# Decoder layer with retention and a mixture of experts: the closing batch's projection to its fifth expert tile reordered, GpSimd's last products and VectorE's early plan rewritten

## The chip, the cores and the metric

One core of one Trainium2 chip runs the whole program. The metric is the device time of one execution in microseconds, as the median of several runs.

## The reference, cut to what matters

The input is x[8, 256, 128]: eight batches of 256 tokens. Three residual blocks follow one another.

```python
x = x + attention(layernorm(x))          # 16 heads of 64, causal, gated by a sigmoid, projected by Wout
x = x + retention(layernorm(x), ctx)     # 16 heads of 8, queries from x, keys and values from ctx
x = x + experts(layernorm(x))            # 12 experts 128 -> 512 -> 128, each token goes to its best 3

gate_logits = einsum('bsd,de->bse', x, Wg)
topw, sel = top_k(gate_logits, 3); topw = softmax(topw)
h = gelu(einsum('bsd,edh->ebsh', x, Wup) + bup)
y = einsum('ebsh,ehd->ebsd', h, Wdown) + bdown
out = einsum('bse,ebsd->bsd', cw, y)     # cw: topw at the chosen experts, 0 elsewhere
```

## The kernel before, in words

The program is written by hand, one instruction stream for each engine, tied by semaphores. It has two phases that overlap.

**Attention phase.** Batch b goes through eight steps s = 0 to 7, one pair of heads each. In one step TensorE does the scores of pair s, the query and key projection of pair s + 1, the turning (transposes) of the probabilities of pair s - 1 (`turn`) and the weighing of the values of pair s - 2 (`weigh`). VectorE takes the maxima of the scores (`maxima`, L1331 and L1332, into `nmx`), the ratios of sums and gates (`ratio`, L1344 to L1351; where `turned()` holds the result is `rg`, L1347, and TensorE transposes it at L983; the last batch does so from pair 2 on), and scales the weighed values (`scale_out`, L1360, into `oT`). ScalarE takes the exponentials (`probs`) and copies out of PSUM. In the same steps the batch before (`prev`) is finished: projection by Wout in step 2, first residual and its normalisation in step 3 (`x1b`, `brs`, `xn2`, L1374 and L1376), the retention state in steps 4 and 5 (`state` on TensorE, `read_state` L1407 on VectorE, `retained` on GpSimd), second residual in step 6 (`x2b`, `xc3`, again L1374 and L1376), logits and the choice of experts in step 7 and in steps 0 and 1 of the next batch (`route_a`, `choose`, `route_b`, `route_c`). Batches 1 to 6 run in a loop on each engine, the last batch (b = 7) is written out.

GpSimd holds what no other engine has time for, in one fixed order: the rotated queries (`queries`, four operations of `rotate`), the rotated keys (`keys`, four operations), the outer products of keys and values for the retention state (`products`, two operations of about 1.95 us, into `kv`, or for the last batch `kv_last`, which lies in `wkv_sb`), the sums of `retained`, the copy of the residual (`keep`), the threefold copy of the tokens (`pack`), and the scatters `send(b, n)`, n = 0 to 5, that write a batch's tokens to `tokens_by_expert` in DRAM, ordered by expert. Between the scatters stand small operations (`carry`) behind waits for VectorE, which place the scatters in time. `v_xc3`, `v_dl`, `v_nm`, `v_norm` are VectorE's semaphores: batch's xc3 ready, logit differences ready, maxima, scaled values.

**Expert phase.** The rows of `tokens_by_expert` are handled in 35 tiles: 24 of 256 rows and 11 of 128. Which expert and which rows a tile has is worked out on VectorE, as plans of small integers: the first 7 tiles (EARLY) from the counts of six batches (`early_plan`), the next 3 from those of seven (`later_plan`), the rest from all. Each plan is a chain of operations on 12 to some 170 numbers, each of which waits for the one before (`link`). Beforehand `early_plan` has three parts, run after steps 2, 3 and 5 of the last batch; the third (`first_rows`, `experts_past`, `tile_rows`, L1591 to L1606) ends with the increment of `v_first`. SyncE waits for it, then loads the tiles (`load(n)`, L440); ahead of that it stores padding rows behind each expert's region, twelve stores of 390 KB (L445).

A tile n is: `turn_tokens(n)` (TensorE, L1166, 2 transposes), a copy of them (ScalarE, `tokens_high`, L877), a copy of the expert's up weights (`up_high`, L872), `up(n)` (TensorE, L1182, 8 matmuls), `gelu(n)` (ScalarE, L855, 4 operations), `down(n)` (TensorE, L1212, 16 matmuls), `results(n)` (VectorE, L1735 and L1738) and `scatter(n)` (GpSimd, L677). up(n) and up(n - 2) share a PSUM bank, so up(n) waits for gelu(n - 2); down(n) waits for gelu(n) and for results of an earlier tile.

Tiles 0 to 4 are interleaved by hand with the end of the last batch, which has no attention left to hide in: projection (L1043), first residual, four retention states (`state(b, t, half)`, L1061 and L1062, two matmuls in all but the first two), their readings, second residual, `ffn_in` (L1075), `logits` (L1081), `counts` (L1091 to L1095), choice. Between them ScalarE must change its function table twice: from gelu's to that of the logarithm and exponential (L897) for the root (L728, L730), and back (L903), each ahead of the next gelu. LAST_CHAIN = 3 says behind which tile this happens.

The order of work that the change touches is written in TensorE's list at the end of its stream, in ScalarE's list behind `LAST_CHAIN`, in GpSimd's `batch`, `first_half` and the lines behind its loop, and in VectorE's lists of `early_plan`, `later_plan` and `results`.

## Time and profile before

| | us |
|---|---|
| median of 3 runs | 491.77 |
| lowest and highest | 487.0, 491.91 |
| the profiled execution | 489.44 |
| its span (first to last instruction) | 487.4 |
| TensorE busy in the span | 440.2 (90%) |
| VectorE | 366.6 (75%) |
| ScalarE | 324.7 (67%) |
| GpSimd | 242.3 (50%) |
| mean granted TensorE clock | 0.97 |

The profile is of one execution. Its times are counted from the first instruction; 2.0 us of the execution's time lie around the span. The last attention batch's steps 2 to 7 lie at about 294 to 333 us, the closing projection to tile 4 at 338 to 375, the other tiles up to 476, and the sum of the results behind that. A timeline row gives start, duration, engine, line, operation, what is written and read with its shape, the count, and in brackets the idle time of the engine before it with what ended it. Rows of a view that merges count their instructions.

### The profile page before, as it was taken

To read this page: it belongs to the slowest core of one execution; us is meant where nothing else is said; L and a number is where in the kernel's file an instruction comes from. 1 tells how busy PE (TensorE), PEld (TensorE's weight loads), DVE (VectorE), ACT (ScalarE), POOL (GpSimd) and SP (SyncE) were. 2 spreads that over 40 slices of the span, in tenths; PEclk is the share of its full clock that TensorE was granted. 3 is DMA by queue.
4 is the path that set the end of the run, shared out by engine and by line. 5 is a ranking of instruction groups with operands and counts; after the bars stand their busy time and mean duration, and the time that the engine had idled before them with its cause. 6 is when DMAs were issued, how large, how long until landed. Compare 5 with 4: busy or idle time off the path is not lost.

```text
span 487.4 us, 12686 instructions
## 1 busy us (share of the span) xinstructions
PE 440.2 (90%) x3562; PEld 366.9 (75%) x3562; DVE 366.6 (75%) x1291; ACT 324.7 (67%) x1041; POOL 242.3 (50%) x368
## 2 busy tenths in 40 slices
PE   6899999999999999999999999858879999888790
PEld 5677877877787887787787787547669998788790
DVE  3876688898898898898889889696776577454357
ACT  3899768776866867876867786434556756564460
POOL 4230042666558358267376565651836566564541
PEclk9999999999999999999999999788989999999896
DMA  8990111112111111111112116972011322211136
GB/s 262 370 279 3 48 26 37 38 46 48 35 49 45 36 46 51 41 42 42 47 35 57 37 36 150 198 124 57 29 50 44 101 78 70 63 48 51 49 109 242
DMA packets 53171, 39.22 MB, mean 80 GB/s; under 512 B 12063, under 2 KB 48723, under 8 KB 53132
## 3 DMA queue, kind: packets, MB, share of 16 engines
q1 hardware_dynamic: 49228, 31.75, 25.7%
q0 software_dynamic: 3472, 6.49, 4.2%
q10 hardware_dynamic: 432, 0.53, 0.3%
q8 instruction: 16, 0.26, 0.3%
q14 instruction: 23, 0.19, 0.1%
HBM read 25.59 MB, written 13.87 MB: 81 GB/s over the span
## 4 chain that ended last, share of the span: by engine, by line
PE 47%; DVE 28%; issue 10%; ACT 5%; DMA 3%; another core or an unknown queue 3%; DVEq 2%; POOL 1%; SPq 0%; ACTq 0%; POOLq 0%
PE zb L922 7%; PE ob L994 5%; PE sc L964 5%; PE xb L1068 5%; DVE scales L1350 4%; DVE nmx L1332 3%; PE ob L1212 3%; PE zb L1212 3%; PE sc L1182 2%; DVE kv_lo L1396 2%; PE tb_a L977 2%; PE tb_b L977 2%; DVE x_all L1804 2%; PE sc L958 2%
## 5 line engine op out<-in xcount | busy, mean ns | idle before, releaser
L677 POOL DMA_INDIRECT results_by_token<-y_sb,row_i x59 | 59.2, 1003 | 48.0 <-DVE y_sb L1738 19.3
L747 ACT ACTIVATE qk<-zb 128x512 f32<-128x512 f32 x64 | 38.2, 596 | 49.1 <-PE zb L922 49.0
L754 ACT ACTIVATE p_sb<-sc,nmx 128x128 f32<-128x128 f32 x128 | 47.6, 372 | 26.0 <-DVE nmx L1332 15.0
L756 ACT ACTIVATE p_sb<-sc,nmx 128x256 f32<-128x256 f32 x128 | 61.7, 482 | 0.0
L597 POOL TENSOR_TENSOR spare_p<-tri 128x1 f32<-128x1 f32 x36 | 7.1, 198 | 104.3 <-DVE xn L1425 66.0
L964 PE MATMUL sc<-qk 64*128 64x256 f32 (+1 forms) x512 | 58.5, 346 | 0.5 <-ACT qk L747 0.5
L994 PE MATMUL ob<-pT,v_sb 128*64 128x256 f32 (+1 forms) x512 | 56.0, 340 | 0.7 <-DVE oT L1360 0.7
L610 POOL DMA_INDIRECT tokens_by_expert<-packed,slot_i x48 | 47.8, 996 | 10.1 <-issue 7.5
L964 PEld LDWEIGHTS sc<-qk 64*128 64x128 f32 x512 | 46.4, 192 | 3.3 <-ACT qk L747 0.6
L994 PEld LDWEIGHTS ob<-pT,v_sb 128*64 128x64 f32 x512 | 31.3, 136 | 19.3 <-issue 8.4
L1332 DVE TENSOR_REDUCE nmx<-sc 128x2 f32<-128x512 f32 x64 | 43.6, 681 | 0.0
L922 PE MATMUL zb<-xT_hi,wqk_hi 128*128 128x256 f32 x112 | 36.6, 327 | 0.0
L855 ACT ACTIVATE hT<-sc,bup_sb 128x256 f32<-128x256 f32 (+1 forms) x72 | 26.4, 441 | 13.3 <-PE sc L1182 4.7
L764 ACT ACTIVATE pT<-tb_a 128x384 f32<-128x384 f32 (+1 forms) x64 | 33.9, 530 | 1.1 <-PE tb_b L983 0.3
L764 ACT ACTIVATE pT<-tb_b 128x384 f32<-128x384 f32 (+1 forms) x64 | 34.5, 538 | 0.0
L1212 PE MATMUL zb<-wdn_all,hT 128*128 x248 | 31.4, 276 | 2.6 <-ACT hT L855 1.4
L977 PE MATMUL tb_a<-ident,p_sb 128*128 128x128 f32 x192 | 32.6, 280 | 0.6 <-ACT pT L764 0.5
L1212 PEld LDWEIGHTS zb<-wdn_all,hT 128*128 128x128 f32 x248 | 29.8, 192 | 3.5 <-issue 3.3
L1212 PE MATMUL ob<-wdn_all,hT 128*128 x224 | 29.9, 286 | 2.7 <-ACT hT L855 2.4
L977 PE MATMUL tb_b<-ident,p_sb 128*128 128x128 f32 x192 | 31.8, 275 | 0.0
L922 PE MATMUL zb<-xT_hi,wqk_lo 128*128 128x256 f32 x112 | 31.6, 282 | 0.0
L922 PE MATMUL zb<-xT_lo,wqk_hi 128*128 128x256 f32 x112 | 31.4, 281 | 0.0
(320 smaller groups left out, 1267.8 us busy)
## 6 DMA issues: line engine op xcount, KB each, us to landing
scaleT<-scale_rows SPq DMA_DIRECT2D x102, 64.0 KB, 2.6
tokens_by_expert<-padding SPq DMA_DIRECT2D x12, 390.0 KB
xg<-tokens_by_expert SPq DMA_DIRECT2D x24, 130.0 KB
wup_all<-in_L_ffn_Wup SPq DMA_DIRECT2D x1, 3072.0 KB, 15.3
wdn_all<-in_L_ffn_Wdown SPq DMA_DIRECT2D x12, 256.0 KB, 4.8
wkv_sb<-in_L_attn_Wkv SPq DMA_DIRECT2D x2, 512.0 KB, 6.6
ctx_b<-in_ctx SPq DMA_DIRECT2D x8, 128.0 KB
results_by_token<-y_sb,row_i POOLq DMA_INDIRECT x59
```

What stands on the lines that cost most here:

```text
L610: pool.indirect_dma_start(out=xs, out_offset=bass.IndirectOffsetOnAxis(ap=slot_i[:, t, k:k + 1], axis=0), in_=packed[:, t, k, :], in_offse ...
L677: pool.indirect_dma_start(out=ys, out_offset=bass.IndirectOffsetOnAxis(ap=row_i[:, u, a:a + 1], axis=0), in_=y_sb[:, u, a, :], in_offset=None,
L747: act.activation(qk[:, :, :].rearrange("p h j -> p (h j)"), zb[:, :], ACT.Copy).then_inc(a_qk, 1)
L754: act.activation(p_sb[:, w, h, 0:P], sc[:, k, S:S + P], ACT.Exp, bias=nmx[:, w, 0, n:n + 1], accum_out=total[:, w, 0, h:h + 1])
L756: act.activation(p_sb[:, w, h, P:3 * P], sc[:, k, 0:S], ACT.Exp, bias=nmx[:, w, 1, n:n + 1], accum_out=total[:, w, 1, h:h + 1]).then_inc(a ...
L764: ins = act.activation(pT[:, s % 2, h, 0:n], tb[h][:, 0:n], ACT.Copy)
L922: ins = pe.matmul(o, lhs[l], rhs[m], start=(n == 0), stop=(last and n == 2), skip_group_check=True)
L964: ins = pe.matmul(sc[:, score_bank(w, h), o:o + n], qk[r, 0, t * P:(t + 1) * P], qk[r, 1, 0:n], start=False, stop=(t == 0), skip_group_che ...
L977: ins = pe.transpose(tb[h][:, k * P:(k + 1) * P], p_sb[:, s % 2, h, k * P:(k + 1) * P], ident[:, :])
L994: ins = pe.matmul(ob[h * DH:(h + 1) * DH, t * P:S], v_sb[:, t, 2 * s + h, :], pT[:, s % 2, h, t * S:(2 + t) * P], start=(t == 0), stop=(t ...
L1212: ins = pe.matmul(ffn_out(n)[:, a * D:(a + 1) * D], hT[:, n % 2, k, a * P:(a + 1) * P], wdn_all[:, bass.ds(e, 1), k, :].rearrange("p a d - ...
L1332: dve.tensor_reduce(nmx[:, w, 1, :], sc[:, w:w + 2, 0:S], AX.X, ALU.max, negate=True).then_inc(v_nm, 1)
```

## The change

Five things change. (1) GpSimd: the last batch's `keys` is called in the batch before the loop's end (batch B - 3, now written out behind a loop that is one shorter), between `send(b, 0)` and `send(b, 1)`; it stood behind the loop. (2) GpSimd: the last batch's outer products are cut into four half operations; the first two wait for `v_xc3`, the other two for `v_dl`, of batch 6; `send(B - 3, 5)` moves ahead of `retained(B - 2, 1)`. (3) VectorE: `early_plan` has five parts, after steps 2, 3, 4, 5 and after the batch; the table of first rows comes from other arithmetic (steps per tile, capped by a minimum), `used` is worked out last; `later_plan` likewise; three constants are set ahead of the loop. (4) TensorE and ScalarE: up(1) stands ahead of down(0), up(2) ahead of down(1), up(3) and the fourth turn ahead of `ffn_in`, down(2) ahead of `logits`, up(4) ahead of `counts`; ScalarE copies tile 4's weights and tokens ahead of its change of table. (5) VectorE: `results(1)` stands ahead of the root's refinement, no longer behind `scale_third`.

```diff
@@ -210,10 +210,13 @@
+        steps_on = moved[:, :, :].rearrange("p a e -> p (a e)")[:, 0:EARLY * (E + 1)].rearrange("p (a e) -> p a e", e=E + 1)
+        tiles_f, capped = eid[:, :].rearrange("p (a n) -> p a n", a=2), rows[:, :].rearrange("p (n a) -> p n a", a=2)
-        used = sb("used", [P, E])
+        used_all = sb("used_all", [P, E + 1])
+        used = used_all[:, 0:E]
@@ -624,9 +627,11 @@
                 carry(2)
                 pool.tensor_copy(x_all[:, bass.ds(tile_of(b, 0), T), :], x2b[:, :, :]).then_inc(p_keep, 1)
 
-            def first_half(b, cur):
+            def first_half(b, cur, between=None):
                 begin(b)
                 send(b, 0)
+                if between is not None:
+                    between()
                 pool.wait_ge(v_norm, at(cur, PAIRS, 1))
                 carry(4)
                 send(b, 1)
@@ -634,7 +639,7 @@
                 carry(5)
                 send(b, 2)
 
-            def batch(b, older):
+            def batch(b, older, between=None):
 
                 queries(b)
                 if older is not None:
@@ -646,22 +651,32 @@
                 keep(b)
                 pack(b)
                 outer(after(b))
-                first_half(b, after(after(b)))
+                first_half(b, after(after(b)), between)
+
+            def last_keys():
+                keys(B - 1, B - 2, 4)
 
             first_outer()
             batch(0, None)
-            with pool.Fori(0, B - 3) as i:
+            with pool.Fori(0, B - 4) as i:
                 batch((i, 1), (i, 0))
-            keys(B - 1, B - 2, 4)
+            batch(B - 3, B - 4, last_keys)
             queries(B - 2, 8)
             send(B - 3, 3)
             retained(B - 2, 0)
             send(B - 3, 4)
+            send(B - 3, 5)
             retained(B - 2, 1)
-            send(B - 3, 5)
-            products(0, kv_last).then_inc(p_kv, 1)
             keep(B - 2)
-            products(1, kv_last).then_inc(p_kv, 1)
+            for t, ready in enumerate((v_xc3, v_dl)):
+                pool.wait_ge(ready, B - 1)
+                for half in range(2):
+                    heads = slice(half * DH, (half + 1) * DH)
+                    k = kt[:, t, heads].rearrange("p (h d) -> p h d", d=RD)
+                    v = ctx_b[:, t, heads].rearrange("p (h e) -> p h e", e=RD)
+                    ins = pool.tensor_tensor(kv_last[:, t, half, :].rearrange("p (h d e) -> p h d e", d=RD, e=RD),
+                                             bc(k, 3, RD), bc(v, 2, RD), ALU.mult)
+                ins.then_inc(p_kv, 1)
             pack(B - 2)
             def ups_ahead(n):
 
@@ -894,6 +909,8 @@
             pT_out(B - 1, PAIRS - 1)
             for n in range(LAST_CHAIN):
                 tile(n)
+            up_high(LAST_CHAIN + 1)
+            tokens_high(LAST_CHAIN + 1)
             act.preload_act_table_set(ROOTS)
             root(B - 1, 1)
             act.wait_ge(pe_XN, B)
@@ -901,7 +918,8 @@
             act.wait_ge(v_dl, B)
             act.activation(el[:, :, :], dl[:, :, :], ACT.Exp).then_inc(a_el, 1)
             act.preload_act_table_set(GELUS)
-            for n in range(LAST_CHAIN, TILES):
+            gelu(LAST_CHAIN)
+            for n in range(LAST_CHAIN + 1, TILES):
                 tile(n)
 
 
@@ -1225,23 +1243,27 @@
             state(b, 0, 0)
             state(b, 0, 1)
             turn_tokens(2)
+            up(1)
             down(0)
-            up(1)
             state(b, 1, 0)
             state(b, 1, 1)
             turn_tokens(3)
+            up(2)
             down(1)
-            up(2)
+            up(3)
+            turn_tokens(4)
             ffn_in(b)
+            down(2)
             logits(b)
-            down(2)
+            up(4)
             counts(None, b)
-            for n in range(LAST_CHAIN, TILES):
+            turn_tokens(5)
+            down(3)
+            for n in range(LAST_CHAIN + 2, TILES):
                 if n + 1 < TILES:
                     turn_tokens(n + 1)
                 up(n)
-                if n > LAST_CHAIN:
-                    down(n - 1)
+                down(n - 1)
             down(TILES - 1)
 
 
@@ -1564,6 +1586,9 @@
                 if n == 0:
                     x_low(0)
             dve.wait_ge(tables_ready, 8)
+            dve.tensor_scalar(steps_on[:, :, E], tau[:, 0:EARLY], float(SLOTS), None, ALU.mult)
+            dve.memset(used_all[:, E:E + 1], 0.0)
+            dve.memset(capped[:, :, 1], float(E * CAP))
             dve.tensor_copy(filled[:, :], region[:, :]).then_inc(v_filled, 1)
             step(0, None, None, None, 0, chain())
             dve.wait_ge(a_wqk, 5)
@@ -1611,14 +1636,27 @@
                     link(dve.tensor_tensor(more[:, :, :], bc(count[:, :], 2, M), bc(steps256[:, :], 1, E), ALU.is_gt))
                     link(dve.tensor_reduce(whole[:, :], more[:, :, :], AX.X, ALU.add))
                 if part == 1:
+                    dve.tensor_scalar(jump[:, :], whole[:, :], float(-SLOTS), float(CAP), ALU.mult, ALU.add)
                     tile_ends(link, whole[:, :])
-                    link(dve.tensor_tensor(ahead[:, :], ends[:, :], whole[:, :], ALU.subtract))
-                    link(dve.tensor_scalar(ahead[:, :], ahead[:, :], -1.0, float(EARLY), ALU.mult, ALU.add))
+                if part == 2:
+                    first_tiles(link, EARLY, first_plan)
+                if part == 3:
+                    last_rows(link, EARLY, first_plan).then_inc(v_first, 1)
+                if part == 4:
+                    link(dve.scalar_tensor_tensor(ahead[:, :], whole[:, :], float(EARLY), ends[:, :], ALU.add, ALU.subtract))
                     link(dve.scalar_tensor_tensor(used[:, :], ahead[:, :], 0.0, whole[:, :], ALU.max, ALU.min))
-                if part == 2:
-                    first_rows(link, whole[:, :], SLOTS)
-                    experts_past(link, EARLY)
-                    tile_rows(link, EARLY, first_plan, SLOTS).then_inc(v_first, 1)
+
+            def first_tiles(link, n, table):
+
+                link(dve.tensor_tensor(past[:, 0:n, :], bc(ends[:, :], 1, n), bc(tau[:, 0:n], 2, E), ALU.is_le))
+                link(dve.tensor_tensor(steps_on[:, 0:n, 0:E], past[:, 0:n, :], bc(jump[:, :], 1, n), ALU.mult))
+                dve.tensor_reduce(tiles_f[:, 1, 0:n], past[:, 0:n, 0:E - 1], AX.X, ALU.add)
+
+            def last_rows(link, n, table):
+
+                link(dve.tensor_reduce(capped[:, 0:n, 0], steps_on[:, 0:n, :], AX.X, ALU.add))
+                link(dve.tensor_reduce(tiles_f[:, 0, 0:n], capped[:, 0:n, :], AX.X, ALU.min))
+                return dve.tensor_copy(table[:, :, :], tiles_f[:, :, 0:n])
 
             def later_plan(part, link):
 
@@ -1626,14 +1664,17 @@
                     link(dve.scalar_tensor_tensor(count[:, :], filled[:, :], float(1 - SLOTS), region[:, :], ALU.add, ALU.subtract))
                     link(dve.tensor_tensor(more[:, :, :], bc(count[:, :], 2, M), bc(steps256[:, :], 1, E), ALU.is_gt))
                     link(dve.tensor_reduce(whole[:, :], more[:, :, :], AX.X, ALU.add))
-                    link(dve.tensor_tensor(tiles_of[:, :], whole[:, :], used[:, :], ALU.subtract))
                     dve.tensor_tensor(parts[:, 1, :], filled[:, :], region[:, :], ALU.subtract)
                 if part == 1:
+                    link(dve.tensor_tensor(tiles_of[:, :], whole[:, :], used[:, :], ALU.subtract))
+                    dve.tensor_tensor(jump[:, :], used_all[:, 1:E + 1], whole[:, :], ALU.subtract)
                     tile_ends(link, tiles_of[:, :])
-                    first_rows(link, whole[:, :], SLOTS)
+                    dve.tensor_scalar(jump[:, :], jump[:, :], float(SLOTS), float(CAP), ALU.mult, ALU.add)
+                    n = NEXT - EARLY
+                    link(dve.scalar_tensor_tensor(steps_on[:, 0:n, E], used_all[:, 0:1].broadcast_to([P, n]), float(SLOTS), steps_on[:, 0:n, E], ALU.mult, ALU.add))
                 if part == 2:
-                    experts_past(link, NEXT - EARLY)
-                    tile_rows(link, NEXT - EARLY, next_plan, SLOTS).then_inc(v_next, 1)
+                    first_tiles(link, NEXT - EARLY, next_plan)
+                    last_rows(link, NEXT - EARLY, next_plan).then_inc(v_next, 1)
                 if part == 3:
                     take(link, NEXT - EARLY)
 
@@ -1746,10 +1787,11 @@
                     dve.tensor_tensor(parts[:, 0, :], filled[:, :], region[:, :], ALU.subtract)
                     dve.tensor_copy(pad_row[:, :], filled[:, :]).then_inc(v_pad, 1)
                 step(b, b - 1, None, None, s, link)
-                if s in (2, 3, 5):
-                    early_plan((2, 3, 5).index(s), link)
+                if s in (2, 3, 4, 5):
+                    early_plan(s - 2, link)
             for s in range(2):
                 step(None, b, None, b - 1, s, link)
+            early_plan(4, link)
             later_plan(0, link)
 
             first_residual(b, link)
@@ -1768,11 +1810,11 @@
                     later_plan(2, link)
             second_residual(b, link)
             tokens(3)
+            results(1)
             deviation(b, 1, link)
             route_a(b, link)
             choose(link)
             scale_third()
-            results(1)
             route_b(b, link)
             route_c(b, link)
             later_plan(3, link)
```

## Rows read from the trace of the kernel before

**Rows 1.** Windows: us; busy (count) of PE, PEld, DVE, ACT, POOL; clock; DMA; GB/s
```profile
254.87:277.27 22.40, 21.79 (x186) 16.72 (x185) 20.05 (x62) 15.85 (x60) 14.83 (x26) 1.00 0.19 46
294.06:329.25 35.19, 26.54 (x191) 20.57 (x191) 29.55 (x73) 16.44 (x59) 21.44 (x32) 0.85 0.88 160
308.00:315.00 7.00, 6.71 (x30) 5.24 (x29) 4.46 (x11) 2.82 (x11) 4.84 (x9) 0.51 1.22 192
325.00:332.00 7.00, 5.87 (x36) 4.98 (x34) 5.73 (x21) 5.28 (x22) 2.44 (x3) 0.52 0.34 84
361.00:366.00 5.00, 4.75 (x30) 4.42 (x31) 4.15 (x27) 2.52 (x4) 1.33 (x4) 0.68 0.33 82
```

**Rows 2.** TensorE's timeline, last batch, steps 3 and 5
```profile
306.79 0.33 PE L983 MATMUL tb_a<-ident,rg 128*128 128x128 f32 x1 [2.82 <-DVE rg L1347]
...
324.12 0.33 PE L983 MATMUL tb_a<-ident,rg 128*128 128x128 f32 x1 [4.04 <-DVE rg L1347]
```

**Rows 3.** VectorE's timeline, the loop's step 3, then the last batch
```profile
261.80 0.48 DVE L1376 TENSOR_SCALAR xn<-x1b,bmv 128x128 f32<-128x128 f32 x2
...
295.00 2.35 DVE L1396 TENSOR_TENSOR kv_lo<-kv,kv_hi 128x1024 fp32r<-128x1024 f32 x2
...
301.40 1.80 DVE L1376 TENSOR_SCALAR xn<-x1b,bmv 128x128 f32<-128x128 f32 x2
...
304.45 0.29 DVE L1615 TENSOR_TENSOR ahead<-ends,whole 128x12 f32<-128x12 f32 x1
...
318.26 0.16 DVE L1591 TENSOR_TENSOR begun<-whole,ends 128x12 f32<-128x12 f32 x1
...
319.79 0.34 DVE L1598 TENSOR_TENSOR moved<-past,jump 128x84 f32<-128x84 f32 x1
...
320.58 2.62 DVE L1604 TENSOR_SCALAR first_plan<-eid 128x7 int32<-128x7 f32 x1
...
323.44 0.17 DVE L1344 RECIPROCAL rr<-total 128x4 f32<-128x4 f32 x1
...
326.37 1.71 DVE L1374 TENSOR_SCALAR brs<-bmv 128x2 f32<-128x2 f32 x1
```

**Rows 4.** GpSimd's timeline, last batch
```profile
301.41 0.74 POOL L536 TENSOR_TENSOR kq<-ctx_b,tab 128x256 f32<-128x256 f32 x1
...
321.20 1.97 POOL L574 TENSOR_TENSOR wkv_sb<-kt,ctx_b 128x1024 f32<-128x1024 f32 x1
...
326.10 1.95 POOL L574 TENSOR_TENSOR wkv_sb<-kt,ctx_b 128x1024 f32<-128x1024 f32 x1
```

**Rows 5.** TensorE's timeline: tile 0's turn, down(0), logits, down(4)
```profile
333.82 0.38 PE L1166 MATMUL sc<-ident,xg 128*128 128x128 f32 x2
...
346.80 2.05 PE L1212 MATMUL zb<-wdn_all,hT 128*128 x16 [1.40 <-ACT hT L855]
...
360.88 0.61 PE L1081 MATMUL xb<-fwg_sb,xn3T 128*128 128x12 f32 x4 [1.77 <-ACT xn3T L900]
...
373.02 2.13 PE L1212 MATMUL ob<-wdn_all,hT 128*128 x16
```

**Rows 6.** The chain that ended last, tiles 5 to 9 (start us, us)
```profile
380.88 1.78 PE ob L1212 x16
...
382.88 1.73 PE sc L1182 x8
```

**Rows 7.** VectorE's waits: 294 to 330 , then the loop's 254.87 to 277.27
```profile
DVE oT L1360 <- PE ob L994: 2.5, 1, 2.5
DVE prod L1407 <- PE xb L1068: 2.1, 3, 1.0
...
DVE prod L1407 <- PE xb L1068: 1.1, 2, 0.6
```

**Rows 8.** ScalarE's timeline: the change of table
```profile
358.74 1.28 ACT L897 ACT_TABLE_LOAD   x1
```

**Rows 9.** SyncE's queue: the padding stores
```profile
297.19 21.19 SPq L445 DMA_DIRECT2D tokens_by_expert<-padding  x12
```

## The prediction

> **What bounds the kernel now.** I read the windows of busy time first, to compare the last attention batch, where the change sits, with the same steps one batch earlier. From the second score maxima to the seventh (steps 2 to 7) the loop's batch takes 22.40 us and the last one 35.19 us [rows 1], though the last one has less to do. In the loop TensorE is busy 21.79 of 22.40 us: the loop is TensorE's. In the last batch TensorE is busy 26.54 of 35.19 and VectorE 29.55: the bound has moved to VectorE, and TensorE waits. TensorE's timeline shows the two large waits, 2.82 us and 4.04 us, both for `rg`, which VectorE makes after its piece of the plan [rows 2]. About a microsecond behind each wait the granted clock drops to about half, that is to 1.2 GHz, for some 7 us (0.51 in 308 to 315 and 0.52 in 325 to 332) [rows 1], so each wait is paid for twice.
>
> VectorE's own timeline, read beside GpSimd's, tells why it is late. Its operations on a dozen numbers take 0.2 to 0.3 us, but three are far longer: `xn` 1.80 for a pair, `first_plan` 2.62, `brs` 1.71 [rows 3]. Each of them lies over a GpSimd product: the last batch's `keys` at 301.41, and the two outer products at 321.20 and 326.10 [rows 4]. first_plan ends at 323.20 and the product over it at 323.17; brs ends at 328.08 and the product over it at 328.05. So here a GpSimd operation holds VectorE up to its end.
>
> Behind the batch, TensorE waits 1.40 and 1.77 us [rows 5] around the closing batch's projection, and the clock falls once more (0.68 in 361 to 366 [rows 1]). From tile 5 on TensorE runs without a gap, 1.73 us for an up, 1.78 for a down [rows 6], so whatever is won ahead of that should arrive at the end.
>
> **The change, part by part.** The yardstick for the batch is the start of the seventh maxima (329.25), for the tail the start of tile 4's down product (373.02 [rows 5]).
>
> (a) `keys` of the last batch moves from before the queries (301.41) to behind the first of GpSimd's scatters, about 295.1, where GpSimd was idle. It stops blocking xn: 1.80 becomes the loop's 0.48 [rows 3], which is 1.3 saved. It now lies beside VectorE's two kv_lo subtractions, 2.35 us from 295.00 [rows 3], both of whose inputs are in SBUF. No row shows these two together. Lower end: 0, if GpSimd is the one that waits. Upper end: 2.5, the whole of keys (four operations from 301.41, the first 0.74 [rows 4]). Since first_plan, which waited already when the product began, lost to it, I take 1.5, and VectorE has no slack behind it. Net −1.3 + 1.5 = +0.2.
>
> The Trainium skill ("SBUF — State Buffer", "Who interferes with whom") says that a VectorE instruction with two SBUF inputs contends with a GpSimd instruction that reads SBUF, and that one in a two-port mode contends with any; by it kv_lo is exposed. The rows so far agree for one-input operations (first_plan, brs). Were only those exposed, the +1.5 here would be 0.
>
> (b) Step 3's plan loses three linked operations after `ends`, the first 0.29 [rows 3], the others stretched to 0.43 beside GpSimd, about 1.2 together with their gaps, and gets one unlinked one (0.1): −1.1.
>
> (c) The plan's last piece, all in step 5, runs from 318.26 to 323.44, 5.2 us [rows 3], and all of TensorE's 4.04 us lies under it. It is now two pieces. The comparison, product and one reduction go to the end of step 4: two at 0.34 [rows 3] and one at 0.24, +0.9. Two reductions and a copy stay in step 5: 0.7. So −5.2 + 0.9 + 0.7 = −3.6. The first products of GpSimd are no longer over them, as they now wait for the closing of the second residual.
>
> (d) Those products, now in four halves of about 1 us (half of 1.95), begin at xc3 (step 6) and at dl (step 7). brs falls from 1.71 to 0.17: −1.5. Against it, rg(6), with two SBUF inputs, comes 0.5 us after xc3: lower end 0, upper 2.0 (both halves), taken 1.3. Net −0.2. In step 7 the same with rg(7) and the choice behind it: 0 to 2.0, taken 1.5; partly paid by the clock, since step 7 before ran at 1.2 GHz (0.5 saved). Net +1.0.
>
> (e) With the 2.82 us wait shortened to well under 1 us I expect no fall of the clock in 308 to 315. VectorE's waits for TensorE there, 2.5 for `ob` and 2.1 for `xb`, should shrink to the loop's at the same steps, 1.1 for `xb` [rows 7] and a little for `ob`: −3.2. Bounds: 0 (the clock falls anyway) to −3.2.
>
> Batch: 0.2 − 1.1 − 3.6 − 0.2 + 1.0 − 3.2 = −6.9, taken as −7.0. A second way: the loop's 22.40, less the two things that it has and the last batch has not (1.4), plus the plan's four pieces (0.8 + 1.0 + 0.9 + 0.7), keys 1.5 and products 1.3, gives 27.2 against 35.19, −8.0, before step 7's +1.0. They agree.
>
> (f) The tail. With up(1) ahead of down(0), the up product runs where TensorE waited 1.4 us for the first gelu. Up to down(4) the same products are issued as before. Counted from 345.4: up(1), down(0), four state products of 2 x 0.86, the third turn, up(2), down(1), up(3), the fourth turn end at 358.0; ScalarE then copies tile 4's tokens (0.4), loads a table (1.28 [rows 8]), takes the root (0.5) and copies xn3T: 360.6. The logits start there, 0.3 us earlier than before, with down(2) already behind them, and TensorE waits 0.4. `dl` comes 1.5 later, then el, a second table load and gelu(3) 1.6: 365.2. TensorE, with up(4), the counts and the fifth turn done at 363.0, waits 2.2 for it. Then down(3) 1.78, a turn 0.2, up(5) 1.73: down(4) at 369.0 instead of 373.02, −4.0. From the waits alone: 1.40 and 1.77 [rows 5] plus 5 us at 0.68 (1.6 lost [rows 1]) less 2.6 of new waits is −2.2, with smaller waits left out. I take −3.5, bounds −1 (the 2.2 us wait brings the clock down for 5 us) to −4.5. results(1) ahead of the route takes 0.9 us off VectorE's way to the slots in a place where it was idle for the root; the second plan is shorter by about 0.3, under the same cover. The extra early piece (two operations, 0.4) lies in VectorE's 0.8 us wait for the projection.
>
> (g) Costs put at nothing: retained(1) now stands behind two scatters, not one, but its input comes later than both; the scatter queue gets its data earlier; the three initial operations before the loop are 0.3 us at most.
>
> Sum: −7.0 − 3.5 = −10.5 on the profiled execution's 489.44 (span 487.4 and 2.0 around it) = 478.9. That execution lies 2.3 under the median of three, 491.77, so the same step from the median is 481.3. I forecast 480.0, between.
>
> **The rivals.**
> 1. The ports take it back. kv_lo waits for all of keys (+2.5), rg(6) and rg(7) for both halves (+2.0 each), and the clock falls once in the batch and once in the tail. Terms: (a) +1.2, (b) −1.1, (c) −3.6, (d) +0.5 and +1.5, (e) −1.6: −3.1, with the tail at −2: −5.1, time 485.5. For it: first_plan lost the port once already. Against it: halves give VectorE a gap each microsecond.
> 2. The padding. SyncE's twelve stores of padding rows start at 297.19 and are issued until 318.4 [rows 9]; 12 x 390 KB at the 192 GB/s of 308 to 315 [rows 1] take 24 us, so the DMA is busy with them until about 322. The first tile's load stands behind them in the same queue, and TensorE turns that tile inside the last batch's last step. It did so at 333.82 [rows 5], 12 us behind that; with the batch 7 us shorter this is 5 us. If the load lands only at 328, the batch's gain stops just under 6 and the time is 481 to 483. Inside my range.
> 3. Slower. The new 2.2 us wait ahead of down(3) stands right before the stretch where TensorE has no gap at all. If the clock falls there and stays at 1.2 GHz, each microsecond of work costs another. The longest low stretches seen are 7 us, price 3.5 us. It decides against the change only if the low stretch exceeds 2 x 10.5 = 21 us; at 30 us the price is 15 and the time 494. Against it: no row has one that long.
> 4. It does nothing: the plan was cover for a wait on something else. Against it: rg is named in both waits, and the loop shows the steps without the plan at 22.40. Time 490.
>
> **How the numbers follow.** Forecast with rival 2 inside it 0.76, rival 1 0.16, rival 3 0.03, rival 4 0.05. About 1% is what a measurement can tell from no change here (the three runs lie 1% apart), so faster means under 486.9. Nearly all of the first and two thirds of rival 1 are: 0.84 faster, 0.12 the same, 0.04 slower. Low end: all terms at their good bounds, about −15: 474. High end 487, where rival 1 ends.
>
> **What would show it.** Right: maxima(2) to maxima(7) takes 26 to 28.5 us; the 4.04 and 2.82 us waits for rg under 1 us; a clock of 1.00 over this stretch; xn near 0.5, no `first_plan` operation above 0.5; kv_lo with one of its two stretched by 0.7 to 2.5; rg(6) about 1.5; down(4) 3 to 4 us nearer to the projection. Wrong: a clock of 0.5 for 5 us or more in steps 4 and 5, or a new wait of TensorE for the first tile's tokens above 2 us.

## The result and the profile after

| | before | after |
|---|---|---|
| median, us | 491.67 (5 runs, 487.0 to 491.91) | 483.98 (5 runs, 482.46 to 489.68) |
| ratio | | 0.9896, 95% interval 0.9854 to 0.9938 |
| the profiled execution | 489.44 | 489.68 |
| its span | 487.4 | 487.7 |

The change makes the kernel faster by 1.0% by the ratio on record. The two medians alone are 7.7 us or 1.6% apart; with five runs each, which spread over 4.9 and 7.2 us, the ratio and its interval are the safer figure. I had forecast 480.0, which is 2.4% under the median of before: the right sign, less than half of the size by the ratio, two thirds of it by the medians, inside the range. The profiled execution of after is the slowest of its five and as long as that of before, although much in it is faster; where it loses that again is what had to be found. Its loop ends 1.14 us later (second maxima at 295.20, before 294.06).

The windows of the kernel after (us; busy and count of PE, PEld, DVE, ACT, POOL; clock; DMA; GB/s), first the batch, then what follows it:

```profile
295.20:321.00 25.80, 23.18 (x194) 17.55 (x193) 23.54 (x68) 16.56 (x59) 21.30 (x32) 1.00 1.00 178
308.00:315.00 7.00, 6.71 (x52) 4.81 (x52) 5.36 (x14) 4.71 (x17) 6.05 (x11) 1.00 1.25 187
326.00:330.00 4.00, 1.40 (x6) 1.01 (x8) 0.58 (x5) 0.63 (x2) 0.00 (x0) 0.51 0.69 151
...
334.00:338.00 4.00, 3.69 (x17) 3.72 (x18) 3.11 (x21) 0.38 (x1) 1.28 (x2) 0.50 0.00 0
...
342.00:374.00 32.00, 27.82 (x166) 22.32 (x164) 24.31 (x112) 19.00 (x44) 19.03 (x28) 1.00 0.13 37
```

The first line stands against 35.19 us in [rows 1]: steps 2 to 7 are 9.4 us shorter. The second line is the stretch that ran at half clock before: the same 6.71 us of TensorE now hold 52 of its instructions instead of 30, at 1.00. Then comes something new: from 326 the clock is 0.5, that is 1.2 GHz, for some 12 us, and no other engine has much to do.

TensorE's timeline says what it is (rows of step 3, the last pair's turn, tile 0's turn, the closing projection, down(0), the logits, down(3), down(4)):

```profile
301.20 0.33 PE L1001 MATMUL tb_a<-ident,rg 128*128 128x128 f32 x1 [0.54 <-DVE rg L1369]
...
324.88 0.52 PE L995 MATMUL tb_a<-ident,p_sb 128*128 128x128 f32 x3 [2.07 <-ACT pT L779]
...
328.60 0.69 PE L1184 MATMUL sc<-ident,xg 128*128 128x128 f32 x2 [2.87 <-DMA xg<-tokens_by_expert]
...
334.31 6.40 PE L1061 MATMUL xb<-wout_sb,oT 128*128 128x128 f32 x32 [0.33 <-DVE filled L1476]
...
345.94 1.95 PE L1230 MATMUL zb<-wdn_all,hT 128*128 x16
...
359.59 0.61 PE L1099 MATMUL xb<-fwg_sb,xn3T 128*128 128x12 f32 x4 [0.20 <-ACT xn3T L917]
...
364.36 2.05 PE L1230 MATMUL zb<-wdn_all,hT 128*128 x16 [1.94 <-ACT hT L870]
368.19 1.95 PE L1230 MATMUL ob<-wdn_all,hT 128*128 x16
```

The two waits for `rg`, 2.82 and 4.04 us in [rows 2], are 0.54 us and none. In their place tile 0's turn, which in [rows 5] waited for nothing, waits 2.87 us for its tokens, right behind another 2.07 us without work. The clock goes down, and the projection takes 6.40 us in place of 3.81. It ends at 340.7 where it ended at 341.7 before: of 9.4 us won, 1.1 went with the later end of the loop, 7.2 between the seventh maxima and here, and 1 is left. The tail is as forecast: no wait at down(0), 0.20 at the logits, 1.94 at down(3), and down(4) is 4.8 us earlier than in [rows 5].

What the load itself waited for stands in the chain that ends at tile 0's turn (start, us, what):

```profile
312.54 9.96 DMA tokens_by_expert<-packed,slot_i
...
322.70 5.86 DMA xg<-tokens_by_expert
```

The first is the last scatter of batch 5's tokens (`send(B - 3, 5)`). The load waits for it in SyncE's list (`dispatched`, L436), beside the plan that I had named as its only condition. The plan was ready at 316.1 and the last padding store issued at 320.1; the scatter had landed only at 322.5, 9.96 us behind its issue. Both transfers run while the mean busy share of the DMA stays near 1.

VectorE of the kernel after, to be read against [rows 3]:

```profile
296.13 3.35 DVE L1418 TENSOR_TENSOR kv_lo<-kv,kv_hi 128x1024 fp32r<-128x1024 f32 x2
...
303.33 0.51 DVE L1398 TENSOR_SCALAR xn<-x1b,bmv 128x128 f32<-128x128 f32 x2
...
315.61 0.45 DVE L1659 CAST first_plan<-eid 128x14 int32<-128x14 f32 x1
...
319.09 0.17 DVE L1396 TENSOR_SCALAR brs<-bmv 128x2 f32<-128x2 f32 x1
...
320.09 0.98 DVE L1369 TENSOR_TENSOR rg<-rr,gate 128x256 f32<-128x256 f32 x1
...
324.01 0.69 DVE L1369 TENSOR_TENSOR rg<-rr,gate 128x256 f32<-128x256 f32 x1
324.62 1.03 DVE L1463 COPY pick<-top 128x6 f32<-128x6 f32 x1
```

and GpSimd's keys and products that lie under them, against [rows 4]:

```profile
296.24 1.70 POOL L539 TENSOR_TENSOR kq<-ctx_b,tab 128x256 f32<-128x256 f32 x1
297.90 1.97 POOL L541 TENSOR_TENSOR kq<-ctx_b,tab 128x128 f32<-128x128 f32 x2
...
319.72 2.28 POOL L677 TENSOR_TENSOR wkv_sb<-kt,ctx_b 128x512 f32<-128x512 f32 x2 [0.87 <-DVE xc L1398]
323.35 2.27 POOL L677 TENSOR_TENSOR wkv_sb<-kt,ctx_b 128x512 f32<-128x512 f32 x2 [1.34 <-DVE dl L1459]
```

xn, first_plan and brs are short again. Beside `keys` the pair of kv_lo is 1.0 us longer and GpSimd's own first operation is 1.70 in place of 0.74. Both lose, and single operations, read in narrower windows, show how:

```profile
296.13 1.22 DVE L1418 TENSOR_TENSOR kv_lo<-kv,kv_hi 128x1024 fp32r<-128x1024 f32 x1
297.26 2.22 DVE L1418 TENSOR_TENSOR kv_lo<-kv,kv_hi 128x1024 fp32r<-128x1024 f32 x1
297.90 0.51 POOL L541 TENSOR_TENSOR kq<-ctx_b,tab 128x128 f32<-128x128 f32 x1
```

Before, each kv_lo took 1.22. Now the first is as long as before, and the GpSimd operation that began 0.1 us behind it is 0.96 longer. The second kv_lo begins while that one runs and is 1.0 longer. The next GpSimd operation takes 0.51, half of the pair's 1.01 in before and so not held, and the one behind it 1.49. The rows read as turns: operation by operation, one engine waits while the other's runs.

SyncE's queue of the kernel after, the padding stores and behind them the first seven loads:

```profile
298.30 21.75 SPq L448 DMA_DIRECT2D tokens_by_expert<-padding  x12
...
322.70 7.77 SPq L443 DMA_DIRECT2D xg<-tokens_by_expert  x7
```

The load is issued at 322.70 and TensorE has the tokens at 328.60. That was my rival 2, with its place right and its price far too low.

### The profile page after: what moved, and what is told of

The parts are those of the page before. It is cut to its first block, busy times and chain, and to the rows that moved or that the text cites. A ratio compares the mean times of both kernels' runs of the same rounds, so it can differ in the third digit from the quotient of the medians.

```text
span 487.7 us, 12664 instructions
## 1 busy us (share of the span) xinstructions
PE 442.4 (91%) x3562; PEld 368.8 (76%) x3562; DVE 360.6 (74%) x1289; ACT 324.1 (66%) x1041; POOL 245.2 (50%) x370
## 3 DMA queue, kind: packets, MB, share of 16 engines
q1 hardware_dynamic: 49228, 31.75, 26.1%
## 4 chain that ended last, share of the span: by engine, by line
PE 52%; DVE 20%; DMA 8%; issue 7%; ACT 5%; another core or an unknown queue 3%; POOL 3%; DVEq 1%; SPq 0%; ACTq 0%; POOLq 0%
PE zb L940 7%; PE ob L1012 6%; PE sc L982 5%; PE zb L1230 4%; PE xb L1086 4%; DVE scales L1372 4%; PE ob L1230 3%; PE sc L1200 3%; DVE nmx L1354 3%; PE xb L1061 2%; DMA tokens_by_expert<-packed,slot_i 2%; DVE kv_lo L1418 2%; PE tb_a L940 2%; PE tb_a L995 2%
## 5 line engine op out<-in xcount | busy, mean ns | idle before, releaser
L982 PE MATMUL sc<-qk 64*128 64x256 f32 (+1 forms) x512 | 57.1, 339 | 0.5 <-ACT qk L762 0.5
L1012 PE MATMUL ob<-pT,v_sb 128*64 128x256 f32 (+1 forms) x512 | 57.1, 345 | 0.4 <-DVE oT L1382 0.4
L982 PEld LDWEIGHTS sc<-qk 64*128 64x128 f32 x512 | 45.1, 187 | 3.2 <-ACT qk L762 0.6
L1230 PE MATMUL zb<-wdn_all,hT 128*128 x248 | 33.0, 284 | 5.4 <-ACT hT L870 4.0
L1230 PEld LDWEIGHTS zb<-wdn_all,hT 128*128 128x128 f32 x248 | 30.9, 199 | 6.9 <-issue 6.7
L1061 PE MATMUL xb<-wout_sb,oT 128*128 128x128 f32 x256 | 32.6, 290 | 0.3 <-DVE filled L1476 0.3
L1230 PE MATMUL ob<-wdn_all,hT 128*128 x224 | 28.7, 277 | 4.1 <-ACT hT L870 2.1
L1061 PEld LDWEIGHTS xb<-wout_sb,oT 128*128 128x128 f32 x256 | 31.8, 206 | 0.7 <-issue 0.7
```

Source lines behind the costliest of these rows:

```text
L982: ins = pe.matmul(sc[:, score_bank(w, h), o:o + n], qk[r, 0, t * P:(t + 1) * P], qk[r, 1, 0:n], start=False, stop=(t == 0), skip_group_che ...
L1012: ins = pe.matmul(ob[h * DH:(h + 1) * DH, t * P:S], v_sb[:, t, 2 * s + h, :], pT[:, s % 2, h, t * S:(2 + t) * P], start=(t == 0), stop=(t ...
L1061: ins = pe.matmul(xb[:, t * P:(t + 1) * P], oT[:, s, t, :], wout_sb[:, s, :], start=(t == 0 and s == 0), stop=(s == PAIRS - 1), skip_group ...
L1230: ins = pe.matmul(ffn_out(n)[:, a * D:(a + 1) * D], hT[:, n % 2, k, a * P:(a + 1) * P], wdn_all[:, bass.ds(e, 1), k, :].rearrange("p a d - ...
```

## The experiments

Fourteen kernels ran, two of them the kernel after unchanged (after_same, after_again) and two the same other kernel (between, between_again). The diffs are against the kernel after unless something else is said. Medians of kernels on different chips are not compared with each other, only with their own kernel before: it had 489.95 beside the first four, 493.74 beside the next four, 491.74 beside the three behind them and 490.03 beside the last three.

### How much is the batch, how much the tail

**after_same** is the kernel after, unchanged, as a yardstick on this chip.

> The changed kernel once more, unaltered, as the standard for the others and to see whether its first profiled execution (489.68 us, five runs' median 483.98) was a typical one. Theory P (the first expert tile's load lands behind the padding stores): 483 to 485 us, TensorE waiting 2 to 3.5 us for xg ahead of the first tile's turn, granted clock about 0.5 behind it, the projection 5 us or more instead of 3.8. Rival Q (that wait belonged to a slow execution only): no such wait in this profile.

**tail_only** is the kernel before with parts 4 and 5 of the change (the orders of TensorE and ScalarE, `results(1)`). **batch_only** is the kernel after without them.

```diff
 tail_only, against the kernel before
-            down(0)
             up(1)
+            down(0)
...
-            down(1)
             up(2)
+            down(1)
+            up(3)
+            turn_tokens(4)
```

> The kernel before, with the order of the tail alone changed (TensorE's and ScalarE's lists, results(1) ahead of the refinement). My terms: the tail is worth 3 to 4 us by itself, 487.5 to 488.5. Rival: the tail's gain is lost again in the tiles behind it, under 1 us, 490.5 to 492.

> The changed kernel with the old order of the tail. Theory P: the batch's 9.4 us shrink to 2 to 5 at the projection's end, time 486.5 to 489. If the forecast's term of 7 were right in full, 484.5 and less. If the two halves add up, this gain plus that of the tail alone is that of the whole change, 7.7.

**warm** gives TensorE something to do while it waits for the tokens:

```diff
                 if b == B - 1 and s == PAIRS - 1:
+                    for _ in range(26):
+                        pe.transpose(zb[:, 0:P], ident[:, :], ident[:, :])
                     turn_tokens(0)
```

> The changed kernel with 26 transposes of the identity into the idle bank zb ahead of the first tile's turn; they fill the wait for its load (some 2.9 us at full clock). Theory P with the clock as its second half: the projection takes 3.7 to 3.8 instead of 6.4 us, 2.5 to 4 us less, 480 to 481.5. Rival: the wait alone costs, the clock does not matter, 484 or slightly more.

| | median, us | ratio to before | interval |
|---|---|---|---|
| after_same | 487.45 | 0.9951 | 0.9907 to 0.9995 |
| tail_only | 486.53 | 0.9917 | 0.9884 to 0.995 |
| batch_only | 490.44 | 0.999 | 0.9949 to 1.0032 |
| warm | 484.87 | 0.9899 | 0.9859 to 0.994 |

By the medians the tail alone is worth 3.4 us, near the 3.5 that I had counted. Its trace is less clean: down(4) is 3.7 us earlier, but 1.5 of that stands ahead of the projection's end (340.2 against 341.7), and from there to down(4) it wins only 2.2 (29.1 us against 31.3). The batch alone, 9 us shorter in the trace, is worth nothing that can be measured. In batch_only and in after_same the first tile's turn waits longer than in the first trace:

```profile
329.02 0.69 PE L1181 MATMUL sc<-ident,xg 128*128 128x128 f32 x2 [4.68 <-DMA xg<-tokens_by_expert]
```

(batch_only), and 4.43 us in after_same. In warm the wait is filled and the projection is back at its old length:

```profile
333.58 3.81 PE L1063 MATMUL xb<-wout_sb,oT 128*128 128x128 f32 x32 [0.58 <-DVE filled L1478]
```

The clock did not stay up, it came back. Warm's windows from the last pair's turn, through the 26 transposes, to tile 0's turn:

```profile
323.00:324.00 1.00, 0.17 (x1) 0.20 (x2) 1.00 (x2) 1.00 (x4) 1.00 (x2) 0.80 1.11 175
324.00:327.00 3.00, 3.00 (x15) 3.00 (x15) 1.24 (x8) 0.31 (x1) 0.57 (x1) 0.50 1.31 109
327.00:330.00 3.00, 2.37 (x22) 2.13 (x21) 0.24 (x2) 0.00 (x0) 0.00 (x0) 1.00 0.97 218
```

It fell ahead of the transposes, behind the 2.07 us without work that TensorE has at the last pair's turn, and was full again behind 3 us. That is worth 2.6 us by the medians against after_same; 484.87 is above the 480 to 481.5 that I expected and nearer to the rival's 484. The wait itself stays: the projection cannot begin before tile 0's turn, which stands ahead of it in TensorE's list.

### Is it the padding ahead of the load

**late0** moves all that waits for tile 0's tokens behind the batch's last work (`turn_tokens(0)` behind the projection, ScalarE's and VectorE's copies likewise).

```diff
-                if b == B - 1 and s == PAIRS - 1:
-                    turn_tokens(0)
...
-            turn_tokens(1)
+            turn_tokens(0)
             project(None, b, range(PAIRS)).then_inc(pe_OUT, 1)
+            turn_tokens(1)
```

> The changed kernel with everything that waits for the first tile's rows moved behind what does not: its turn on TensorE from the last pair's turn to ahead of the projection, ScalarE's copy of it behind the last pair's, VectorE's copies of its rows behind the choice. Theory P: the wait for the load is met 2 to 3 us later, about 1 us of it stays and the clock does not fall: the projection's start 2 to 4 us earlier than in the changed kernel, 481 to 483 where that took 484 to 487. Rival (something else in the last step holds the projection): within 1 us of the changed kernel.

**between** changes only the order of SyncE's issues:

```diff
-            with sp.Fori(0, E) as i:
+            pads(0, 10)
...
             sp.wait_ge(v_first, 1)
-            for n in range(EARLY):
+            for n in range(2):
                 load(n)
+            pads(10, E)
+            for n in range(2, EARLY):
+                load(n)
```

> The changed kernel with SyncE's first two tile loads between the tenth and the eleventh of the twelve padding stores; the same bytes, another order. Theory P: the first tile's rows land at 323 to 325 instead of 328.6 to 329, TensorE's wait of 2.9 to 4.4 us goes, the projection starts at 329 to 331 instead of 334.3 and takes 3.8 us: 4 to 6 us less than the changed kernel, 479 to 482. Rival: what holds the first load is SyncE's own issue or the scatters, not the stores ahead in the queue: no change.

**between_late** is both together.

> Both of the two others of this set at once. Theory P: no more than the load's new place alone, within 1 us of it, as then nothing waits for the rows. Rival (rows still late): 1 to 3 us better than either.

| | median, us | ratio to before | interval |
|---|---|---|---|
| late0 | 483.17 | 0.9811 | 0.9732 to 0.989 |
| between | 481.44 | 0.9763 | 0.9677 to 0.9849 |
| between_late | 483.0 | 0.9797 | 0.969 to 0.9904 |

Late0 has no wait of TensorE for the tokens, and its projection ends at 334.2, 6.0 us earlier than in after_same. But my expectation that its clock would not fall was wrong: from 326 to 331 it is 0.50, and the projection takes 5.16 us. So the token wait is not needed for the fall.

```profile
326.00:331.00 5.00, 4.22 (x24) 3.15 (x22) 3.30 (x21) 1.01 (x2) 1.08 (x3) 0.50 0.34 86
```

SyncE's queue in between:

```profile
319.79 1.57 SPq L443 DMA_DIRECT2D xg<-tokens_by_expert  x2
322.26 2.24 SPq L449 DMA_DIRECT2D tokens_by_expert<-padding  x2
```

and TensorE's timeline there, tile 0's turn, the projection and down(4):

```profile
324.09 0.38 PE L1189 MATMUL sc<-ident,xg 128*128 128x128 f32 x2
...
329.00 3.81 PE L1066 MATMUL xb<-wout_sb,oT 128*128 128x128 f32 x32 [0.58 <-DVE filled L1481]
...
360.28 1.97 PE L1235 MATMUL ob<-wdn_all,hT 128*128 x16
```

The load is issued about 2 us earlier than in after_same (321.69) and is there 4.7 us earlier or more, with no wait; the clock does not fall; the projection ends at 332.8 in place of 340.3 and down(4) starts 7.5 us earlier than in after_same (367.75). The ten stores were issued by 313.1, but the load still waited for the scatter of batch 5, which was issued at 311.08 and had landed at 319.7; in after_same it was issued at 311.21 and landed at 321.5. So with two stores fewer ahead the scatter, too, is about 1.7 us shorter, and the load is not held up behind it. The queue order alone gives back what had been lost behind the batch. Taking the wait away from the turn as well (between_late) adds nothing, as it should if nothing waits there any more. The medians of the three kernels, four runs each, are within 1.8 us and their intervals overlap, so they are not ranked among each other. Which of the things ahead of or beside the load delays it, the last two stores or the five other loads, between does not tell apart, since it moves the first two loads ahead of both.

**after_again** and **between_again** are the two kernels once more, side by side on one chip, in five rounds.

> The kernel after, unchanged, beside between_again on one chip. Expected by both theories: 0.985 to 0.995 of before, as in its two comparisons so far; a first load that lands at 327 to 329, TensorE waiting 2.5 to 4.7 us for it.

> The kernel with the first two loads between the tenth and eleventh padding store, unchanged, beside after_again on one chip. If the first tile's load is the step that my prediction missed, it is faster than after_again by the 7.5 us at down(4) less what the gaps in tiles 5 to 20 take back (about 3), that is 4 to 6 us or about 1%, with 0.975 to 0.985 of before. If the first comparison was the chip's, both are within 0.4% of each other.

After: 486.92 us (0.9928, 0.9889 to 0.9966). Between: 481.11 us (0.9829, 0.9778 to 0.9879). The difference, 5.8 us by the medians and 1.0% by the ratios, is what the load's place is worth at the end, inside the 4 to 6 us that I expected. The way there is another: in this pair down(4) is only 4.7 us earlier (after_again waits 2.24 us for the tokens, not 4.4), and the tiles add 3.7 instead of taking back 3. In between_again the clock was 0.52 from 325 to 328.5, again without a wait for tokens, but full before the projection, which takes 3.81 us. This is the best version found, ahead of both kernels.

### The ports, one by one

**keys_back** puts the last batch's keys behind the loop again, **products_back** the products to their old places, whole and without waits; one execution each.

```diff
 keys_back
-            batch(B - 3, B - 4, last_keys)
+            batch(B - 3, B - 4)
+            last_keys()
 products_back
+            products(0, kv_last).then_inc(p_kv, 1)
             keep(B - 2)
+            products(1, kv_last).then_inc(p_kv, 1)
-            for t, ready in enumerate((v_xc3, v_dl)):
...
```

> The changed kernel with the last batch's keys at their old place, behind the loop. From the second to the seventh maxima the changed kernel took 25.8 us in two executions. My term (a) says keys beside kv_lo cost 1.5 and keys beside xn 1.3, so 25.6. The trace of the changed kernel showed kv_lo at 3.35 instead of 2.35, so 1.0 and not 1.5: then 26.1. Rival (keys cost nothing where they now are): 27.1.

> The kernel after with its outer products where they were, whole and without their waits, one ahead of the copy of the residual and one behind it. By my terms (d) the halves save 0.2 us in step 6 and cost 1.0 in step 7, so maxima(2) to maxima(7) should be within 1 us of the 25.8 of the kernel after. By the trace of before, where they lay over first_plan (2.62) and brs (1.71), they would now lie over step 5's piece of the plan and brs: 25.8 + 1.6 to 3 = 27.4 to 28.8.

keys_back: steps 2 to 7 take 26.84 us, 1.0 more than after (487.2 us in all). That is nearer to the rival's 27.1, by which the new place costs nothing, than to the 26.1 that the two rows give. Two further rows are longer in the old place, step 3's brs (0.35, after 0.17) and rg (0.75, after 0.56). Its two rows on VectorE show both sides of the bargain, kv_lo short and xn long:

```profile
294.89 2.35 DVE L1419 TENSOR_TENSOR kv_lo<-kv,kv_hi 128x1024 fp32r<-128x1024 f32 x2
...
301.30 1.80 DVE L1399 TENSOR_SCALAR xn<-x1b,bmv 128x128 f32<-128x128 f32 x2
```

products_back: maxima at 293.91 and 321.67, 27.76 us, 2.0 more than after (486.03 us in all). There the products lie over the second residual:

```profile
316.33 1.62 DVE L1433 SCALAR_TENSOR_TENSOR x2b<-ret,brs,x1b 128x128 f32<-128x128 f32 x2
...
318.79 1.70 DVE L1389 TENSOR_SCALAR brs<-bmv 128x2 f32<-128x2 f32 x1
```

so the part of the change that cuts and delays them is worth 2 us up to the seventh maxima. I had given it 0.2 in (d) and an unpriced share of (c). Both are single executions; what they show is the length of these rows, not a time.

### Where the rest goes: tiles 5 to 24

The table is from the starts of down(4) and of tile 24's turn on TensorE's timeline. Between them stand the same products in every kernel.

The last two columns are TensorE's busy time and the granted clock in that stretch.

| | down(4) | tile 24's turn | between | span | busy | clock |
|---|---|---|---|---|---|---|
| before | 373.02 | 442.74 | 69.7 | 487.4 | 64.05 | 1.00 |
| batch_only | 370.31 | 439.99 | 69.7 | 484.6 | 63.99 | 1.00 |
| tail_only | 369.34 | 440.55 | 71.2 | 485.7 | 63.79 | 1.00 |
| after_same | 367.75 | 439.95 | 72.2 | 486.0 | 63.71 | 1.00 |
| after | 368.19 | 442.49 | 74.3 | 487.7 | 66.26 | 0.95 |
| after_again | 365.40 | 442.16 | 76.8 | 485.7 | 69.38 | 0.91 |
| between_again | 360.71 | 433.74 | 73.0 | 479.1 | 64.57 | 1.00 |
| between | 360.28 | 435.38 | 75.1 | 480.6 | 66.81 | 0.95 |

Between wins 12.7 us at down(4) and 6.8 in the span. In the profiled execution of after, the 4.8 us won at down(4) are gone by tile 24. The table splits the 4.6 us of this stretch: 2.2 are a longer busy time, where the clock fell, and 2.4 are waits. The largest wait comes first, just behind the new tail, and before has none there:

```profile
374.12 2.05 PE L1230 MATMUL zb<-wdn_all,hT 128*128 x16 [2.04 <-ACT hT L870]
```

That is down(5), waiting for ScalarE's gelu. This wait is 1.35 to 2.09 us in after, after_same, after_again, between, between_again and keys_back, 0.5 to 0.6 in late0, between_late, products_back, shift and shift_half, and absent in before, tail_only, batch_only, between_old_tail and warm. ScalarE begins that gelu in after at 372.41, behind 3.3 us without work, though up(5), which it reads, had ended at 368.4; what holds ScalarE is not shown. So a part of what the new order wins at down(4) is paid back one product later.

The rest is in stretches like this one of the kernel after, inside one down product:

```profile
401.41 0.61 PE L1230 MATMUL ob<-wdn_all,hT 128*128 x4 [1.03 <-issue]
402.84 0.61 PE L1230 MATMUL ob<-wdn_all,hT 128*128 x4 [0.81 <-issue]
405.06 0.66 PE L1184 MATMUL sc<-ident,xg 128*128 128x128 f32 x2 [1.62 <-DVE wup_lo L1760]
```

The product has begun, and "issue" says that the profile shows nothing that it waits for. The clock of this kernel in 402 to 407 is 0.76, so such a gap is paid for twice, like the waits.

**between_old_tail** is batch_only with the loads of between. It asks whose the loss is.

> batch_only (the new batch with the old order of the tail) with the first two loads between the tenth and the eleventh padding store. It tells whose the loss in tiles 5 to 20 is. Theory T: it belongs to the new order of the tail, in which up products stand further ahead; with the old order the way from down(4) to the last tile stays at 74 to 75 us as in the kernel before and in batch_only, the gain at down(4) (5 to 7 us against batch_only, from the load that no longer waits) arrives whole, span 478 to 480, time 482 to 484. Theory G: it comes with any gain made ahead of tile 5, since TensorE has to wait at certain places of its own list for the instructions themselves; then the way from down(4) to the last is 77 us or more, with a gap inside the down products of tile 12 or 13 that batch_only has not, and the time is 485 to 487.

486.37 us, 0.9875 (0.98 to 0.995). down(4) starts at 363.80, 6.5 us earlier than in batch_only, and tile 24's turn at 438.00, 2.0 earlier: 74.2 between them. The span is 484.2, in batch_only 484.6. So theory T fell: the old order of the tail loses it too, though less than the 77 us that theory G asked for. One place of it, TensorE's timeline beside the turn of tile 14:

```profile
395.27 0.48 PE L1232 MATMUL ob<-wdn_all,hT 128*128 x2 [1.05 <-issue]
396.00 0.36 PE L1232 MATMUL ob<-wdn_all,hT 128*128 x1 [0.25 <-issue]
```

and its windows, the gap and then the clock:

```profile
395.00:400.00 5.00, 2.83 (x15) 2.41 (x16) 2.85 (x13) 2.70 (x7) 2.52 (x3) 0.79 0.10 34
400.00:405.00 5.00, 5.00 (x27) 5.00 (x26) 3.24 (x16) 2.27 (x6) 1.71 (x3) 0.53 0.28 77
```

batch_only has no such gap there (in 390 to 400 its clock is 1.00 and TensorE is busy 9.75 of 10 us). Gaps at tile 19's turn are in every kernel, before too (0.32, 0.47 and 0.43 us from 423.56). Gaps of 0.4 us or more at the turns of tiles 12 to 14 are in all kernels but before, batch_only, tail_only and warm.

**shift** and **shift_half** ask whether these are places in TensorE's list of instructions, by products added at its very start.

```diff
-            keep_warm(28)
+            keep_warm(20)
+            for _ in range(108):
+                pe.matmul(tb[0][:, 0:16], ident[:, :], ident[:, 0:16], start=True, stop=True, skip_group_check=True)
```

(shift; shift_half keeps the 28 and has 60 of the new ones.)

> The kernel after with 100 more instructions on TensorE at the very start of its stream, ahead of the first batch (108 products of 16 columns in place of 8 transposes, all while it waits for the first tokens; the start may be up to 3 us later). Theory I (instructions come late at places that are fixed in the stream): every gap inside straight-line code moves by about 100 of the 26 products per tile, that is three to four tiles earlier: from the down product beside tile 19's turn to one beside tile 15 or 16, and from tile 28 to 24 or 25. Theory D (gaps belong to what the tile does or to the moment, a DMA or a shared buffer): they stay at tiles 19 and 28. The time is the kernel after's, 484 to 488, plus what the start is later.

> The kernel after with 60 more products (120 instructions with their weight loads) on TensorE at the start of its stream; start about 9 us later. Theory I (places fixed in the list of instructions, in pieces of about 256): the gap of tile 19's turn moves by half a piece, to a tile about two earlier or two to three later, and so does the one at 28. Theory D (it belongs to the tile or to what the others do then): gaps inside the down product beside tile 19's turn and at tile 28 stay there. Time, the kernel after's and 8 to 12 us.

Their times are 524.39 and 510.3 us, far more than I expected. Each of these products is two matmuls on TensorE, so shift has 216 more less 8, and they take 0.12 us each as long as the clock is 1.00 and 0.21 at 0.50; the first batch starts that much later (its first transposes in shift at 48.73 us), and nothing else is meant by these times. The list is moved by 208 and 120 matmuls, twice what I had written down. The gap at tile 19 does not move. Shift, at the turn of tile 19:

```profile
458.05 0.50 PE L1232 MATMUL zb<-wdn_all,hT 128*128 x3
458.86 0.35 PE L1232 MATMUL zb<-wdn_all,hT 128*128 x1 [0.31 <-issue]
460.27 1.09 PE L1232 MATMUL zb<-wdn_all,hT 128*128 x4 [1.06 <-issue]
```

It is the same down product as in before, and the gap stands behind its third matmul there too, 35 us later in the span. Shift has another at tile 13, shift_half has them at tiles 14 and 19. So they belong neither to a moment nor to a fixed distance from the start of the list; theory I fell as well. Theory D held for tile 19; what the tiles 12 to 14, 19 and 28 have in common stays open. A late supply of instructions is not excluded (the profile has a queue, q8, that carries instructions in pieces of 16 KB, none of them from 80 to 280 us, where the loop runs, and one each 10 to 20 us in the tiles), but no run shows it.

## Why the prediction was wrong

Point by point, by its own steps.

- **What bounds the batch: right.** Of both waits for `rg` 0.54 us are left, and the clock stayed at 1.00.
- **(a) keys: right.** xn 0.51 (forecast 0.48), kv_lo +1.0 (taken 1.5, bounds 0 and 2.5). keys_back shows the trade as 1.0 us in favour of the new place, where I had 0.2 against it. The Trainium skill ("SBUF — State Buffer", "Who interferes with whom") says that a VectorE instruction with two SBUF inputs contends with a GpSimd one that reads SBUF; kv_lo agrees. It also calls the shared ports an exclusive lock and says that the order of issue decides who blocks. The single operations agree: the first kv_lo kept its 1.22 us and the keys operation behind it went from 0.74 to 1.70, then the second kv_lo went to 2.22.
- **(b) and (c) the plan: right** as far as the rows go. first_plan's longest row 0.45, the wait of 4.04 us gone; no run takes (b) or (c) by itself.
- **(d) the products: step 7 right, step 6 too low.** brs 0.17 as forecast; rg(6) 0.98 against 0.56 in step 5, so +0.4 where I took 1.3; rg(7) and pick together 1.1 more than before, where I took 1.5. products_back makes the products' new form and place 2 us better than the old one.
- **(e) the clock: right.** It stayed at 1.00, VectorE's wait of 2.5 us for `ob` went, and its waits for `xb` fell from 2.1 to 1.5, forecast 1.1: 3.1 us in all for the 3.2 taken.
- **The batch's sum: −7.0 forecast, −9.4 measured.** With what was measured in (a), −1.3 + 1.0, and in (d), −1.5 + 0.4, and the forecast's −1.1, −3.6 and −3.2 for the others, it is −9.3. That this meets the 9.4 is in part luck: three of the five terms are still forecasts, and keys_back and products_back put −1.0 and −2.0 on what stands here with −0.3 and −1.1. Step 7's +1.0 did not belong in it: it lies behind the seventh maxima.
- **(f) the tail: right up to down(4).** From the end of the projection to down(4) 27.5 us in after (340.7 to 368.2) and in between, 31.3 before: −3.8 for the −3.5 taken. down(3) waits 1.94 for the forecast 2.2. tail_only measured −3.4 by the medians, −2.2 in its trace. But down(4) was a flattering yardstick: down(5) waits 2.04 us in after, so that from the end of the projection to down(5) only 1.8 us are won (33.4 against 35.3).
- **The load (rival 2): the step that failed first.** I had the DMA done by about 322 and gave the first load until 328 at worst, and priced that as 1 us of the batch's 7. The time was right: TensorE had the tokens at 328.60 in after and 328.84 in after_same. The price was not, for four reasons. The load was never held by the stores' issue or the plan alone: it also waits for the last scatter of batch 5, which took 9.96 us among the padding, so it was issued at 322.70, and then took 5.86 us itself. The turn stands ahead of the projection in TensorE's list, so its wait (2.2 to 4.7 us) is paid in full. The clock was low around it, which made the projection 0.5 to 2.6 us longer in after, its repeats and batch_only; what starts the fall is not the token wait alone, as late0 shows. And the DMA was not done at 322: the loads of seven tiles stand in the same queue, and the share of busy DMA stays near 1 until 328, where in before it fell at 323 and was 0 from 325, ahead of the load's issue at 326.01. At down(4) this cost 7.5 us (after_same against between, on two chips) and 4.7 (after_again against between_again, side by side), of which my sum had none and my rival a little over 1. I had compared the load with the turn's old time less 7; I did not ask what the queue would look like once the load, too, came 3 to 4 us earlier.
- **"From tile 5 on TensorE runs without a gap, so whatever is won ahead of that should arrive at the end": the second step that failed.** The kernel before is idle for 5.7 of the 69.7 us from down(4) to tile 24: gaps at tile 19, and named waits of 0.76 us for a gelu at tile 14 and of 1.01 and 1.16 us at the turns of tiles 18 and 20; there is a further gap at tile 28. I had not looked: [rows 6] shows tiles 5 to 9 only. What is won ahead is partly taken back there: 1.5 us in tail_only, 2.5 to 7 in the three traces of after, 5.4 in between, by the table's third column. Beside before, the runs show three things: the wait at down(5) under the new order, longer gaps at tiles 12 to 19, and a clock of 0.91 to 0.95 in three of the five traces. That the last two come also with the old tail order is shown by between_old_tail (0.93); their cause is open.
- **Rival 1 (ports)** did not happen; its loss of 0.5 to 2.5 us per place was at most 1.1. **Rival 3**: in after the wait at down(3) did not bring the clock down (1.00 in 342 to 374). That was luck: behind the same 1.94 us it fell to 0.76 over 365 to 372 in tail_only and to 0.66 over the 5 us beside down(3) in warm, late0, between_late and products_back. **Rival 4** is excluded by the batch's trace.

So in the profiled execution the forecast's −10.5 became −9.4 for the batch, +1.1 for the later loop, +7.2 from the seventh maxima to the projection's end, where the load and the clock are, and −3.8 for the tail: −4.8 at down(4), of which 0.3 is left at tile 24. The other four runs were faster, and the gain by the ratio is real. That the time fell inside the range owes something to luck: the batch gave more than I had promised, and the largest loss stood in my text as a rival priced at a seventh to a fifth of what it was.

## What to carry to other kernels

When a stretch of code becomes shorter, list what must have arrived at its end, and price each transfer from its own issue: the stores ahead of it and the loads behind it in its queue, every semaphore that its issue waits for, and how full the DMA is just then. Here the transfer that it waited for, a scatter, was the longer of the two (9.96 us). If the load is late by a few us, the engine's wait comes at full price, and the clock may be low around it: a wait of 4.4 us went with a loss of 7.5, one of 2.2 with 4.7. The cure here was not faster work but two loads issued ahead of two stores.

Read the whole stretch that you call gapless before you promise that a gain passes through it.
